# Attention on one core: value matmuls of two steps side by side in every second step, and a ring of 16 tiles of exponentials

## The chip, the core and the metric

The kernel runs on one core of one Trainium2 chip. A core has five engines that work at the same time, each on a queue of its own and in the order of that queue: TensorE (PE, matrix multiplication), VectorE (DVE), ScalarE (ACT), GpSimd (POOL) and SyncE (SP, which issues the transfers). They meet through semaphores: an instruction waits until another engine has counted far enough. The metric is the device time of one execution in microseconds (us); lower is better.

## What is computed

Two layers act on 16 images of 32 channels and 64 by 64 pixels. The first is a capsule layer with routing, the second a transformer block on 3x3 patches; each begins with a group normalization and adds its result to its input. The change lies in the attention of the second layer. Cut to that:

```python
xr = x @ Wr.T                                   # patches of 288 numbers to 144
qkv = (xr @ Wqkv.T).reshape(B, N, 3, 8, 18)     # 8 heads of 18 numbers
q, k, v = (qkv[i].reshape(B, 8, 4, n, 18) for i in range(3))   # 4 chunks of n = 1024 pixels
attn = softmax(einsum('bhcnd,bhcmd->bhcnm', q, k) * 18 ** -0.5)
o = einsum('bhcnm,bhcmd->bhcnd', attn, v)
out = o.reshape(B, N, 144) @ Wp.T + bp
```

## The kernel before

The program is five phases with a barrier behind each: a normalization, the routing, a normalization, the attention and a last phase for the MLP and the folding of the patches. Only `attention_phase` is touched.

**Units and steps.** The attention works through 64 units, one for each image and chunk (16 x 4). A unit is 32 steps: 2 groups of four heads ("quads") x 2 halves of 512 queries x 8 blocks of 128 keys. In step t, PE makes four score matmuls (`score`, x = 0 to 3, one per head, 128 keys x 512 queries, bf16), ACT makes the exponentials of each (`exponentials`), and the value matmuls (`values`) multiply these four tiles of exponentials by the values of their heads and add them up in `po`. The value matmuls are f32 and have 32 columns each, so the four stand beside each other in the array, each in a quarter of its columns; the trace shows eight matmul rows for one call. Before the scores of a unit, the greatest score of each row must be known, so the kernel makes every score twice: in each step PE also makes four matmuls for the maxima of the unit after it (`maximum`), and DVE reduces each of them (`TENSOR_REDUCE`).

**The order on PE** is written out by hand in `unit`: score 0, maximum 0, score 1, maximum 1, score 2, maximum 2, the value matmuls of the step before, score 3, maximum 3, and then the task of this step, if it has one. Here a "block" is what stands between maximum 2 and score 3.

**Tasks** are the rest of the work of a unit, laid by a table on certain steps (a unit that it belongs to, its kind, its number):

```python
TASKS = {0: (0, "max", 1), 1: (-1, "turn", 3), 2: (-1, "back", 3),
         3: (-1, "out", 2), 4: (-1, "out", 3), 5: (-1, "out", 4),
         6: (2, "qk", 0), 7: (2, "qk", 1), 8: (2, "qk", 2), 9: (0, "turn", 0), 10: (0, "back", 0),
         11: (2, "qk", 3), 12: (2, "qk", 4), 14: (1, "v", 0), 15: (1, "v", 1),
         16: (1, "v", 2), 17: (0, "turn", 1), 18: (0, "back", 1), 19: (1, "max", 0),
         25: (0, "turn", 2), 26: (0, "back", 2), 27: (0, "out", 0), 28: (0, "out", 1)}
```

So steps 13, 20 to 24 and 29 to 31 have no task. All tasks write one PSUM tile, `pm`, and PE starts a task only when the reader of the task before has taken `pm` out (`reader_before`, and the table `readers` above it). For "turn", "back", "out" and "qk" that reader is DVE, for "v" and "max" it is ACT. DVE does its part of the task of step t-1 in step t, between the second and the third reduction (`if x == 1: task(p, t - 1, which)` in DVE's `unit`).

**Buffers between the engines.** Scores go through 3 PSUM tiles (`sc`), maxima through 3 others (`mp`): the score with number k waits until the exponential of number k - 3 is done, the maximum with number k until the reduction of number k - 3 is done (`bank_before`). The exponentials lie in a ring of 8 tiles of 512 f32 (`ex`), two steps' worth; the first exponential of step t waits until the value matmuls of step t - 2 are done. Every eighth step ACT also copies `po` out into `oc` (`outputs`, L1429), behind the four exponentials of that step; the next value matmuls that start `po` anew wait for it.

Of the kernel before, what the change touches and what calls it, by code (L numbers as in the profile page):

```python
# [951 lines left out]
QUAD = 4  # L952
QUADS = HEADS // QUAD
STEPS = QUADS * QB * KB
# [5 lines left out]
NPART = 3  # L960
BANKS = 3
PER_UNIT = QUAD * STEPS


def bank_before(k):

    if k >= BANKS:
        return k - BANKS + 1
    return max(j for j in range(PER_UNIT - BANKS, PER_UNIT) if j % BANKS == k % BANKS) - PER_UNIT + 1

# [22 lines left out]
def offset(p, d):  # L993

    for _ in range(abs(d)):
        p = p.to(1 if d > 0 else -1)
    return p


def attention_phase(nc, ctx, sems, halves, ln_halves, mixed, moments, w_r, w_qkv, w_p, consts):  # L1000
# [10 lines left out]
    def sb(n, shape, dt=F32):  # L1011
        return ctx.enter_context(nc.sbuf_tensor(f"a_{n}", shape, dt))

    def sem(n):
        sems.append(nc.alloc_semaphore(f"a_{n}"))
        return sems[-1]
# [20 lines left out]
    mleft = sb("mleft", [128, 2, QUAD * KB])  # L1037
    mparts = sb("mparts", [128, NPART, QUAD * KB], BF16)
    mrow = sb("mrow", [NPART * QUAD * KB, 128], BF16)
    RING = 2 * QUAD  # L1040
    ex = sb("ex", [128, RING, CHUNK])
    oc = sb("oc", [128, CHUNK])
    rz = sb("rz", [128, BLK * QUAD])
# [41 lines left out]
    valued = Signal(sem("valued"), STEPS)  # L1085
# [15 lines left out]
    def piece(k, part):  # L1101

        if k == OUTS - 1:
            return packed[:, part, :]
        return pieces[:, k % WIDE, part, CHUNK * (k // WIDE):CHUNK * (k // WIDE + 1)]

    def width(k):
        return NARROW if k == OUTS - 1 else CHUNK
# [136 lines left out]
    def _(pe):  # L1245
# [69 lines left out]
        def score(p, t, x):  # L1315

            quad, qb, kb = t // 16, t // 8 % 2, t % 8
            k = QUAD * t + x
            head = QUAD * quad + x
            if t % 16 == 0 and x == 0:  # L1320
                pe.wait_ge(neg_in[quad].sem, neg_in[quad].at(p.n, 16))

            if not (isinstance(p.n, int) and p.n == 0 and k < BANKS):
                pe.wait_ge(exped.sem, exped.at(p.n, bank_before(k)))
            pe.matmul(sc[k % BANKS][:, :], ks[0:KROWS + NPART, p.h, head, 128 * kb:128 * kb + 128],  # L1325
                      qs[0:KROWS + NPART, p.h, head, CHUNK * qb:CHUNK * qb + CHUNK],
                      start=True, stop=True).then_inc(score_made.sem, 1)

        def maximum(p, t, x):

            k = 4 * t + x
            head, q = divmod(k // 2, KB)
            half = x % 2
            if k % (2 * QUAD * KB) == 0:
                pe.wait_ge(stack_in[head // QUAD].sem, stack_in[head // QUAD].at(p.n, 16 * 12))
            pe.wait_ge(maxed.sem, maxed.at(p.n, bank_before(k)))
            pe.matmul(mp[k % BANKS][:, :], qs[0:KROWS, p.h, head, 128 * q:128 * q + 128],  # L1337
                      ks[0:KROWS, p.h, head, CHUNK * half:CHUNK * half + CHUNK],
                      start=True, stop=True).then_inc(max_made.sem, 1)

        def values(p, t):

            quad, qb, kb = t // 16, t // 8 % 2, t % 8
            g = t // 8
            pe.wait_ge(exped.sem, exped.at(p.n, QUAD * t + QUAD))
            if t == 0:
                pe.wait_ge(v_done.sem, v_done.at(p.n, 3))
            if kb == 0 and not (isinstance(p.n, int) and p.n == 0 and g == 0):
                pe.wait_ge(o_copied.sem, o_copied.at(p.n, g))
            for x in range(QUAD):  # L1350
                last = pe.matmul(po[32 * x:32 * x + 32, :], va[:, p.h, kb, QUAD * quad + x, :],  # L1351
                                 ex[:, (QUAD * t + x) % RING, :], start=kb == 0, stop=kb == KB - 1,
                                 tile_position=(0, 32 * x))
            last.then_inc(valued.sem, 1)

        def unit(p, which):
            for t in range(STEPS):
                for x in range(QUAD):
                    if 0 in which:
                        score(p, t, x)  # L1360
                    if 1 in which:
                        maximum(p.to(1), t, x)
                    if x == 2 and t == 0 and -1 in which:
                        values(p.to(-1), STEPS - 1)
                    elif x == 2 and t and 0 in which:
                        values(p, t - 1)
                task(p, t, which)

        run_units(pe, units, unit)

    @block.scalar
    def _(act):
        for sig in (*t1_stored, spared, neg_spared, *mo_stored):
            act.sem_inc(sig.sem, sig.base)
        nc.scalar.preload_act_table_set(EXP_LN)
        for i in range(3):
            act.wait_ge(combined, i + 1)
            nc.scalar.copy(wc[:, i, :], pm[0:R, 0:3 * C2]).then_inc(wc_copied, 1)
        act.wait_ge(prepared, 1)

        def task(p, t, which):
            if t not in TASKS or TASKS[t][0] not in which:
                return
            d, kind, k = TASKS[t]
            own = offset(p, d)
            if kind == "qk":
                if k == 0:
                    act.wait_ge(spared.sem, spared.at(own.n, 0))
                act.wait_ge(qk_made.sem, qk_made.at(own.n, k + 1))
                nc.scalar.copy(piece(k, 0), pm[:, 0:width(k)]).then_inc(lead.sem, 1)  # L1390
            elif kind == "v":
                nb = min(3, KB - 3 * k)
                act.wait_ge(v_made.sem, v_made.at(own.n, k + 1))
                nc.scalar.copy(va[:, own.h, 3 * k:3 * k + nb, :, 0:HD],
                               pm[:, 0:C2 * nb].rearrange("p (b h d) -> p b h d", h=HEADS, d=HD)).then_inc(v_done.sem, 1)
            elif kind == "max":
                act.wait_ge(neg_turned.sem, neg_turned.at(own.n, k + 1))
                act.wait_ge(neg_spared.sem, neg_spared.at(own.n, 16 * k))
                nc.scalar.copy(mrow[:, :], pm_b[0:96, 0:128]).then_inc(neg_copied.sem, 1)

        def late_task(p, t, which):

            if t not in TASKS or TASKS[t][0] not in which:
                return
            d, kind, k = TASKS[t]
            own = offset(p, d)
            if kind == "qk":
                act.wait_ge(remain.sem, remain.at(own.n, k + 1))
                nc.scalar.copy(piece(k, 1), left[:, k % 2, 0:width(k)]).then_inc(second.sem, 1)  # L1409
            elif kind == "out":  # L1410
                act.wait_ge(t1_done.sem, t1_done.at(own.n, k + 1))
                if not (isinstance(own.n, int) and own.n == 0 and k == 0):
                    act.wait_ge(sq_done.sem, sq_done.at(own.n, k))
                nc.scalar.activation(sqr[:, 0:width(k)], t1[:, k, 0:width(k)], ACT.Square,
                                     accum_out=mo[:, own.h, OUTS + k:OUTS + k + 1]).then_inc(sq_done.sem, 1)

        def exponentials(p, t, pair):
            for x in range(2 * pair, 2 * pair + 2):
                k = QUAD * t + x
                act.wait_ge(score_made.sem, score_made.at(p.n, k + 1))  # L1420
                if x == 0 and not (isinstance(p.n, int) and p.n == 0 and t < 2):
                    act.wait_ge(valued.sem, valued.at(p.n, t - 1))
                nc.scalar.activation(ex[:, k % RING, :], sc[k % BANKS][:, :], ACT.Exp, scale=scale).then_inc(exped.sem, 1)  # L1423

        def outputs(p, g):
            act.wait_ge(valued.sem, valued.at(p.n, 8 * g + 8))
            if not (isinstance(p.n, int) and p.n == 0 and g == 0):
                act.wait_ge(o_normed.sem, o_normed.at(p.n, g))
            nc.scalar.copy(oc[:, :], po[:, :]).then_inc(o_copied.sem, 1)  # L1429

        def unit(p, which):
            for t in range(STEPS):
                if 0 in which:
                    exponentials(p, t, 0)
                    exponentials(p, t, 1)
                if t == 0 and -1 in which:
                    outputs(p.to(-1), 3)
                elif t and t % 8 == 0 and 0 in which:
                    outputs(p, t // 8 - 1)
                late_task(p, t - 1, which)  # L1440
                task(p, t, which)

        run_units(act, units, unit)
# [461 lines left out]
```

## Time and profile before

| | |
|---|---|
| median of 3 runs | 13064.68 us (13056.39 to 13068.2) |
| the profiled execution | 13060.79 us, span 13059.0 us |
| PE busy over the span | 12449.1 us, 95% |
| DVE busy | 9722.8 us, 74% |
| ACT busy | 7866.5 us, 60% |
| first and last value matmul | 4547.9 and 12248.0 us from the span's start |
| mean granted clock of PE | 0.982 of 2.4 GHz |

Busy time counts a matmul from its start to its modelled end, and matmuls overlap, so 95% does not say that PE streams data 95% of the time. In the rows below, the start of a matmul and the start of the next one tell what the first one costs; a duration is longer than that, by the time in which a result drains. The same holds in a lesser measure for DVE and ACT, whose next instruction starts before the end of the one before.

### The profile page before, as it was taken

How to read it: one execution, taken by the hardware profiler on the slowest of the kernel's cores; microseconds unless marked ns; L12 is line 12 of the kernel's file. 1: busy time of each engine (PE TensorE's matmuls, PEld its weight loads, DVE VectorE, ACT ScalarE, POOL GpSimd, SP SyncE). 2: the span in 40 equal slices, each digit the busy share in tenths (PEclk: the TensorE clock that was granted, in tenths of full speed). 3: DMA queues.
4: the chain of work that ended last, by engine and by line, in shares of the span. 5: the costliest groups of instructions: out<-in, count | busy, mean ns of one | idle time of the engine just before them, and what ended most of it. 6: DMA issues, size and time to landing. Idle time of an engine off the chain costs nothing. (4 is left out here: it accounts for less than half of the span.)

```text
span 13059.0 us, 258656 instructions
## 1 busy us (share of the span) xinstructions
PE 12449.1 (95%) x76092; PEld 5276.3 (40%) x76348; DVE 9722.8 (74%) x18034; ACT 7866.5 (60%) x14774; POOL 2684.0 (21%) x2692
## 2 busy tenths in 40 slices
PE   6999999999996499999999999999999999999899
PEld 3555555555553133333333333333333333333233
DVE  7888888888887577777777777777777777777311
ACT  4666666666665166666666666666666666666411
POOL 3454444544443000000000000000000000000143
PEclk9999999999998699999999999999999999999999
DMA  3101011010112523223222232332322323223255
GB/s 77 22 15 22 17 20 22 15 22 15 22 21 55 132 64 75 66 66 73 66 70 69 67 72 66 73 70 64 75 66 67 72 66 71 68 69 72 64 124 109
DMA packets 853225, 771.45 MB, mean 59 GB/s; under 512 B 587076, under 2 KB 621348, under 8 KB 840740
## 3 DMA queue, kind: packets, MB, share of 16 engines
q1 hardware_dynamic: 850468, 747.29, 25.4%
q8 instruction: 703, 11.52, 0.4%
q10 hardware_dynamic: 1536, 8.39, 0.3%
q14 instruction: 518, 4.24, 0.1%
HBM read 510.50 MB, written 244.96 MB: 58 GB/s over the span
## 5 line engine op out<-in xcount | busy, mean ns | idle before, releaser
L1503 DVE TENSOR_REDUCE a_big<-a_mp 128x1 f32<-128x512 f32 x8192 | 5222.3, 685 | 1816.0 <-PE a_mp L1337 1797.7
L1423 ACT ACTIVATE a_ex<-a_sc 128x512 f32<-128x512 f32 x8192 | 4426.4, 601 | 1937.6 <-PE a_sc L1325 1932.6
L1337 PE MATMUL a_mp<-a_ks,a_qs 108*128 108x512 bf16 x8192 | 3131.1, 383 | 39.9 <-DMA a_ks<-qk_parts 25.1
L1325 PE MATMUL a_sc<-a_qs,a_ks 111*128 111x512 bf16 x8192 | 3124.5, 383 | 6.8 <-ACT a_ex L1423 4.5
L849 DVE TENSOR_TENSOR r_prod<-r_pg,r_win 128x512 f32<-128x512 f32 x3584 | 2319.4, 683 | 416.5 <-PE r_pg L583 227.9
L1351 PE MATMUL a_po<-a_ex,a_va 128*32 128x512 f32 x16384 | 2183.0, 605 | 2.1 <-ACT a_oc L1429 0.7
L1239 POOL TENSOR_TENSOR a_pieces<-a_left,a_pieces 128x512 bf16<-128x512 f32 x256 | 295.5, 1154 | 7319.5 <-ACT a_pieces L1409 7319.5
L1325 PEld LDWEIGHTS a_sc<-a_qs,a_ks 111*128 111x128 bf16 x8192 | 794.9, 97 | 2477.6 <-ACT a_ex L1423 1767.0
L524 POOL TENSOR_TENSOR r_prod<-r_temp,r_win 128x512 f32<-128x512 f32 x1024 | 1214.7, 1207 | 1298.3 <-PE r_pl L632 568.3
L587 PE MATMUL r_pg<-r_ident,r_spread 128*128 128x128 f32 x9216 | 1196.7, 278 | 113.3 <-DVE r_prod L849 94.5
L587 PEld LDWEIGHTS r_pg<-r_ident,r_spread 128*128 128x128 f32 x9216 | 1004.9, 142 | 573.0 <-DVE r_prod L849 275.1
L1337 PEld LDWEIGHTS a_mp<-a_ks,a_qs 108*128 108x128 bf16 x8192 | 803.2, 98 | 913.6 <-DVE a_big L1503 237.7
L807 ACT ACTIVATE r_spread<-r_low 128x2048 f32<-128x2048 f32 x512 | 952.1, 1916 | 0.0
L582 PE MATMUL r_pg<-r_stack,r_wv 96*128 96x512 bf16 x2304 | 882.3, 383 | 28.4 <-DVE r_prod L849 10.1
L583 PE MATMUL r_pg<-r_stack,r_wv 128*128 128x512 bf16 x2048 | 778.4, 380 | 0.0
L1269 PE MATMUL a_pm<-a_zw,a_wc 96*128 96x512 f32 x1536 | 711.1, 599 | 15.1 <-DVE a_left L1473 13.4
L1351 PEld LDWEIGHTS a_po<-a_ex,a_va 128*32 128x32 f32 x16384 | 322.5, 107 | 824.7 <-ACT a_ex L1423 702.6
L629 PE MATMUL r_ps<-r_prod,r_ws 128*32 128x512 f32 x4096 | 553.3, 613 | 22.8 <-DVE r_prod L849 15.6
L1808 DVE TENSOR_TENSOR f_u<-f_pw,f_three 96x512 f32<-96x512 f32 x128 | 87.9, 687 | 651.4 <-PE f_pw L1677 650.1
L790 ACT COPY r_temp<-r_pg 128x512 f32<-128x512 f32 x1024 | 544.1, 583 | 20.4 <-ACT r_out_t L775 20.4
L632 PE MATMUL r_pl<-r_prod,r_pick 128*32 128x512 f32 x4096 | 541.1, 600 | 5.3 <-DVE r_prod L849 0.3
L1723 ACT ACTIVATE f_hidden<-f_ph,f_coef 72x512 f32<-72x512 f32 x128 | 99.0, 773 | 652.2 <-PE f_ph L1667 652.2
(192 smaller groups left out, 11795.2 us busy)
## 6 DMA issues: line engine op xcount, KB each, us to landing
a_qs<-qk_parts SPq DMA_DIRECT2D x768, 144.0 KB
a_ks<-qk_parts SPq DMA_DIRECT2D x768, 144.0 KB
qk_parts<-a_pieces SPq DMA_DIRECT2D x128, 768.0 KB, 5.0
f_t<-mixed SPq DMA_DIRECT2D x48, 1536.0 KB, 16.7
a_tw<-second SPq DMA_DIRECT2D x512, 128.0 KB, 3.1
mixed<-a_t SPq DMA_DIRECT2D x256, 256.0 KB, 2.1
r_win<-first SPq DMA_DIRECT2D x128, 280.5 KB, 5.2
a_zw<-layered SPq DMA_DIRECT2D x192, 144.0 KB, 12.2
```

The costliest lines, as they stand in the source:

```text
L524: nc.gpsimd.tensor_tensor(prod[:, g, :].rearrange("p (a b) -> p a b", b=IMG), temp[:, rank, :].rearrange("p (a b) -> p a b", b=IMG), tap_a ...
L582: pe.matmul(bank[:, :], wv_0[0:96, w], stack[0:96, lane, :], start=True, stop=False)
L583: last = pe.matmul(bank[:, :], wv_12[:, w], stack[:, lane, :], start=False, stop=True)
L587: last = pe.transpose(bank[:, 128 * b:128 * b + 128], spread[:, lane, 16 * kk:16 * kk + 16, :].rearrange("p a b -> p (a b)"), ident[:, :])
L807: nc.scalar.activation(to[:, :, half, :], src[:, :, half].unsqueeze(3).to_broadcast([128, BLK, 64, CLEN]), ACT.Exp).then_inc(prob[r].sem, 1)
L849: nc.vector.tensor_tensor(prod[:, g, :].rearrange("p (a b) -> p a b", b=IMG), pg[use % RINGS][:, :].rearrange("p (a b) -> p a b", b=IMG), ...
L1269: last = pe.matmul(pm[:, :], wc[:, i, 128 * (k % WIDE):128 * (k % WIDE) + 128], zw[:, own.h, first:first + CHUNK], start=i == 0, stop=i == 2)
L1325: pe.matmul(sc[k % BANKS][:, :], ks[0:KROWS + NPART, p.h, head, 128 * kb:128 * kb + 128], qs[0:KROWS + NPART, p.h, head, CHUNK * qb:CHUNK ...
L1337: pe.matmul(mp[k % BANKS][:, :], qs[0:KROWS, p.h, head, 128 * q:128 * q + 128], ks[0:KROWS, p.h, head, CHUNK * half:CHUNK * half + CHUNK], ...
L1351: last = pe.matmul(po[32 * x:32 * x + 32, :], va[:, p.h, kb, QUAD * quad + x, :], ex[:, (QUAD * t + x) % RING, :], start=kb == 0, stop=kb ...
L1423: nc.scalar.activation(ex[:, k % RING, :], sc[k % BANKS][:, :], ACT.Exp, scale=scale).then_inc(exped.sem, 1)
L1503: nc.vector.tensor_reduce(big[:, x % 2, k // 2:k // 2 + 1], mp[k % BANKS][:, :], AX_X, ALU.max).then_inc(maxed.sem, 1)
```

## The change

The value matmuls no longer stand in every step. In every even step t the block now holds those of steps t - 2 and t - 1, one after the other; in an odd step nothing stands between maximum 2 and score 3. For the last two steps of a unit they stand in step 0 of the next. The ring of exponentials has 16 tiles in place of 8 (four steps' worth), and the first exponential of step t now waits for the value matmuls of step t - 4. What is multiplied and in which order it is added up in `po` stays, and so do the orders of DVE, POOL and SP. ACT's order stays but for its waits.

```diff
+BATCH = 2
+RING_STEPS = 2 * BATCH
-    RING = 2 * QUAD
+    RING = RING_STEPS * QUAD
                     if x == 2 and t == 0 and -1 in which:
-                        values(p.to(-1), STEPS - 1)
-                    elif x == 2 and t and 0 in which:
-                        values(p, t - 1)
+                        for done in range(STEPS - BATCH, STEPS):
+                            values(p.to(-1), done)
+                    elif x == 2 and t and t % BATCH == 0 and 0 in which:
+                        for done in range(t - BATCH, t):
+                            values(p, done)
-                if x == 0 and not (isinstance(p.n, int) and p.n == 0 and t < 2):
-                    act.wait_ge(valued.sem, valued.at(p.n, t - 1))
+                if x == 0 and not (isinstance(p.n, int) and p.n == 0 and t < RING_STEPS):
+                    act.wait_ge(valued.sem, valued.at(p.n, t - RING_STEPS + 1))
```

In the orders below, L1325 and L1337 of before are L1327 and L1339 of after, and so on, since the change adds two lines above them (four on DVE and ACT); a_sc, a_mp, a_po, a_pm are the PSUM tiles `sc`, `mp`, `po`, `pm`, the digit behind `sc` and `mp` is the buffer.

PE before, from the task "out" of step 4 to the task "out" of step 5:

```order
L1305 MATMUL a_pm<-a_on,a_wp 128x512 x2
L1325 MATMUL a_sc2<-a_qs,a_ks 128x512
L1337 MATMUL a_mp2<-a_ks,a_qs 128x512
L1325 MATMUL a_sc0<-a_qs,a_ks 128x512
L1337 MATMUL a_mp0<-a_ks,a_qs 128x512
L1325 MATMUL a_sc1<-a_qs,a_ks 128x512
L1337 MATMUL a_mp1<-a_ks,a_qs 128x512
L1351 MATMUL a_po<-a_ex,a_va 32x512 x4
L1325 MATMUL a_sc2<-a_qs,a_ks 128x512
L1337 MATMUL a_mp2<-a_ks,a_qs 128x512
L1310 MATMUL a_pm<-a_on,a_wp 32x256 x8
```

PE after, the same place:

```order
L1307 MATMUL a_pm<-a_on,a_wp 128x512 x2
L1327 MATMUL a_sc2<-a_qs,a_ks 128x512
L1339 MATMUL a_mp2<-a_ks,a_qs 128x512
L1327 MATMUL a_sc0<-a_qs,a_ks 128x512
L1339 MATMUL a_mp0<-a_ks,a_qs 128x512
L1327 MATMUL a_sc1<-a_qs,a_ks 128x512
L1339 MATMUL a_mp1<-a_ks,a_qs 128x512
L1327 MATMUL a_sc2<-a_qs,a_ks 128x512
L1339 MATMUL a_mp2<-a_ks,a_qs 128x512
L1312 MATMUL a_pm<-a_on,a_wp 32x256 x8
```

The block of the odd step is gone, and eight score and maximum matmuls are all that stands between two tasks.

DVE at the same place, before: its part of the task of step 4, between the reductions of step 5.

```order
L1503 TENSOR_REDUCE a_big<-a_mp2 128x1
L1503 TENSOR_REDUCE a_big<-a_mp0 128x1
L1496 SCALAR_TENSOR_TENSOR a_t1,a_mo<-a_pm,a_tw 128x512
L1503 TENSOR_REDUCE a_big<-a_mp1 128x1
L1503 TENSOR_REDUCE a_big<-a_mp2 128x1
```

And after:

```order
L1507 TENSOR_REDUCE a_big<-a_mp2 128x1
L1507 TENSOR_REDUCE a_big<-a_mp0 128x1
L1500 SCALAR_TENSOR_TENSOR a_t1,a_mo<-a_pm,a_tw 128x512
L1507 TENSOR_REDUCE a_big<-a_mp1 128x1
L1507 TENSOR_REDUCE a_big<-a_mp2 128x1
```

Nothing moved on DVE: the part of the task still stands behind the second reduction of the step after it.

PE before in steps 20 and 21, which have no task, from block to block:

```order
L1351 MATMUL a_po<-a_ex,a_va 32x512 x4
L1325 MATMUL a_sc2<-a_qs,a_ks 128x512
L1337 MATMUL a_mp2<-a_ks,a_qs 128x512
L1325 MATMUL a_sc0<-a_qs,a_ks 128x512
L1337 MATMUL a_mp0<-a_ks,a_qs 128x512
L1325 MATMUL a_sc1<-a_qs,a_ks 128x512
L1337 MATMUL a_mp1<-a_ks,a_qs 128x512
L1325 MATMUL a_sc2<-a_qs,a_ks 128x512
L1337 MATMUL a_mp2<-a_ks,a_qs 128x512
L1351 MATMUL a_po<-a_ex,a_va 32x512 x4
```

And after, from the block of step 20 on:

```order
L1353 MATMUL a_po<-a_ex,a_va 32x512 x8
L1327 MATMUL a_sc2<-a_qs,a_ks 128x512
L1339 MATMUL a_mp2<-a_ks,a_qs 128x512
L1327 MATMUL a_sc0<-a_qs,a_ks 128x512
L1339 MATMUL a_mp0<-a_ks,a_qs 128x512
L1327 MATMUL a_sc1<-a_qs,a_ks 128x512
L1339 MATMUL a_mp1<-a_ks,a_qs 128x512
L1327 MATMUL a_sc2<-a_qs,a_ks 128x512
L1339 MATMUL a_mp2<-a_ks,a_qs 128x512
L1327 MATMUL a_sc0<-a_qs,a_ks 128x512
L1339 MATMUL a_mp0<-a_ks,a_qs 128x512
```

Eight calls stand together in place of four, and eight pairs of a score and a maximum follow before the next block (three more than shown) in place of four.

## Rows read from the trace of the kernel before

**Rows 1.** The page: busy time, share of the span, instructions of each engine.

```profile
PE 12449.1 (95%) x76092; PEld 5276.3 (40%) x76348; DVE 9722.8 (74%) x18034; ACT 7866.5 (60%) x14774; POOL 2684.0 (21%) x2692
```

**Rows 2.** Windows: length, busy time by engine (instructions), clock, DMA share, GB/s.

```profile
4520.00:4540.00 20.00, 20.00 (x35) 3.54 (x34) 20.00 (x35) 0.00 (x0) 0.00 (x0) 0.50 0.60 112
6000.00:12000.00 6000.00, 5991.48 (x33365) 2278.24 (x33365) 4562.04 (x8162) 3924.10 (x7766) 264.36 (x250) 1.00 0.30 69
```

**Rows 3.** Waits from 6000 to 12000 us: total, times, longest.

```profile
PE a_mp L1337 <- DVE a_big L1503: 6.8, 24, 0.3
```

**Rows 4.** Groups, 6000 to 12000 us: count, busy us, mean ns, idle before.

```profile
L1423 ACT ACTIVATE a_ex<-a_sc 128x512 f32<-128x512 f32 x6327 | 3420.5, 601 | 1489.1 <-PE a_sc L1325 1485.9
```

**Rows 5.** Timeline, a step without a task: start, us, engine, line, what, how many.

```profile
8138.66 0.38 PE L1337 MATMUL a_mp<-a_ks,a_qs 108*128 108x512 bf16 x1
8138.97 1.06 PE L1351 MATMUL a_po<-a_ex,a_va 128*32 128x512 f32 x8
8139.96 0.39 PE L1325 MATMUL a_sc<-a_qs,a_ks 111*128 111x512 bf16 x1
8140.19 0.38 PE L1337 MATMUL a_mp<-a_ks,a_qs 108*128 108x512 bf16 x1
8140.39 2.09 ACT L1423 ACTIVATE a_ex<-a_sc 128x512 f32<-128x512 f32 x4 [0.76 <-PE a_sc L1325]
8140.61 1.89 DVE L1503 TENSOR_REDUCE a_big<-a_mp 128x1 f32<-128x512 f32 x3 [0.36 <-PE a_mp L1337]
...
8141.28 0.38 PE L1325 MATMUL a_sc<-a_qs,a_ks 111*128 111x512 bf16 x1
8141.50 0.38 PE L1337 MATMUL a_mp<-a_ks,a_qs 108*128 108x512 bf16 x1
8141.81 0.64 PE L1351 MATMUL a_po<-a_ex,a_va 128*32 128x512 f32 x4
```

**Rows 6.** Timeline of PE around a task "qk" of three groups of four.

```profile
8106.22 0.38 PE L1337 MATMUL a_mp<-a_ks,a_qs 108*128 108x512 bf16 x1
8106.53 1.50 PE L1274 MATMUL a_pm<-a_zw,a_wc 96*32 96x256 f32 x24
8107.97 0.39 PE L1325 MATMUL a_sc<-a_qs,a_ks 111*128 111x512 bf16 x1
```

**Rows 7.** Timeline, from the task "out" of step 3 to that of step 4.

```profile
8037.50 1.88 PE L1305 MATMUL a_pm<-a_on,a_wp 128*128 128x512 f32 x4
...
8039.22 0.38 PE L1325 MATMUL a_sc<-a_qs,a_ks 111*128 111x512 bf16 x1
...
8039.85 1.29 DVE L1503 TENSOR_REDUCE a_big<-a_mp 128x1 f32<-128x512 f32 x2 [1.46 <-PE a_mp L1337]
...
8041.06 0.68 DVE L1496 SCALAR_TENSOR_TENSOR a_t<-a_pm,a_tw 128x512 f32<-128x512 f32 x1
...
8042.06 1.45 PE L1305 MATMUL a_pm<-a_on,a_wp 128*128 128x512 f32 x3
```

**Rows 8.** Timeline, first units, where PE makes maxima and tasks alone.

```profile
4469.47 0.68 DVE L1473 TENSOR_TENSOR a_left<-a_pm,a_pieces 128x512 f32<-128x512 f32 x1
...
4470.21 2.84 PE L1269 MATMUL a_pm<-a_zw,a_wc 96*128 96x512 f32 x6 [0.77 <-DVE a_left L1473]
...
4473.31 1.29 DVE L1503 TENSOR_REDUCE a_big<-a_mp 128x1 f32<-128x512 f32 x2 [1.96 <-PE a_mp L1337]
...
4474.06 0.39 PE L1337 MATMUL a_mp<-a_ks,a_qs 108*128 108x512 bf16 x1 [0.36 <-DVE a_big L1503]
```

**Rows 9.** Timeline of PE: the same task "qk" without a wait ahead.

```profile
8083.60 2.74 PE L1269 MATMUL a_pm<-a_zw,a_wc 96*128 96x512 f32 x6
```

**Rows 10.** Timeline of ACT around a copy of `po`.

```profile
8028.06 0.60 ACT L1423 ACTIVATE a_ex<-a_sc 128x512 f32<-128x512 f32 x1 [0.76 <-PE a_sc L1325]
8028.56 0.58 ACT L1429 COPY a_oc<-a_po 128x512 f32<-128x512 f32 x1
8029.02 1.60 ACT L1423 ACTIVATE a_ex<-a_sc 128x512 f32<-128x512 f32 x3
```

## The prediction

> **What bounds the kernel now.** I read the page first: PE is busy for 95% of the span [rows 1]. The windows say the same of the stretch that the change touches, which is the attention in its steady part: 5991 of 6000 us, at a granted clock of 1.00, which is 2.4 GHz [rows 2]. Of the waits, those of PE for DVE come to 6.8 us in 6000 [rows 3], so nothing else ends last there. The 6327 exponentials in that window, at 128 per unit, make 121.4 us per unit [rows 4]. Whoever takes time off PE's queue gains it, so long as ACT and DVE still keep up; whoever lets PE wait loses it.
>
> The timeline of a step without a task gives the prices. A score and a maximum start .22 us apart [rows 5], so a pair costs .44. From the last maximum ahead of a block to the score behind it 1.30 us pass (.31 + .99), of which .22 are that maximum, so a block costs 1.08 to 1.09. The step has four pairs and one block, and takes 2.84 [rows 5]. How much of the block is streaming follows from a task "out": two f32 calls of the same 512 columns take 1.72 us (8037.50 to 8039.22) [rows 7], .86 for one. The four value matmuls lie side by side and stream together, so they need .86 once, and about .23 of a block is a price for entering and leaving it.
>
> **The change: what it saves.** Two blocks become one with twice the streaming. Whether the price is then paid once or twice shows in the task "qk" that has three groups of four such matmuls in a row: 1.75 us from the maximum ahead to the score behind, less .22, is 1.53 [rows 6]. Half the columns take half of .86, so three groups stream for 1.29, and .24 is left for all three. The price is paid per stay, not per group, and each pair of steps saves .23: 32 steps x 64 units / 2 = 1024 times, or 236 us. That would be 12,825 us.
>
> The three groups of [rows 6] leave no room for a pause between one and the next: 1.29 of streaming and .24 are all of it. The Trainium skill ("TensorE: Matmul & The Clock Gate", section "Part 3: Packing small matmuls — row/col tiling", The mechanism) says that loading weights overlaps with matmuls in flight only when they use other rows of the array; the groups here all use the same 128 rows. By that rule the second group would pay for its entry again and the saving would be 0 in place of 236; the trace disagrees, with .24 for three groups of half the width.
>
> **What it adds: a wait for the one tile of the tasks.** All tasks write `pm`, and the next one starts only when the one before has been read, for most kinds by DVE, behind its second reduction of the next step. Rows 7 show one such step from its start S, the end of the task "out" of step 3 (8039.22): DVE reduces from S + .63, each .605 after the last, takes `pm` out from S + 1.84 and is done at S + 2.52. PE comes to the next task at S + 2.84. The wait is hidden by .32, and what hides it is the block. In an odd step of the changed kernel the block is gone: PE is there at S + 2.84 - 1.09 = S + 1.75. It may go on .06 after DVE's end (4473.31 + 1.29 - .60 = 4474.00 for a reduction, 4474.06 for the maximum that waited for it [rows 8]), so at S + 2.58. That is a wait of .83. DVE can't be sooner: its two reductions depend on maxima that PE makes in that same step, and it was idle before them (1.46 us in [rows 7]). Behind PE's wait stand the scores and maxima of the next step, so ACT and DVE wait with it and nothing makes it up. Starting again costs something too: the six matmuls of a task "qk" take 2.84 when PE had to wait for `pm` [rows 8], and 2.74 when not [rows 9]. With this .10 one wait costs .93.
>
> By the table, an odd step with a task whose predecessor stands in the step before and is read by DVE is 3, 5, 7, 9, 11, 19 and 27: seven per unit. (15 and 17 follow a "v", 1 a "max", both read by ACT, which is quicker; 25 follows no task.) Without the first two of the first unit, the three that hang on "qk" in the next to last, and all seven of the last, which has no maxima to reduce, 436 are left: 436 x .93 = 405 us.
>
> **What it adds: bursts that three tiles can't hold.** Between blocks there now stand eight pairs in place of four. PE makes one in .44, DVE reduces one in .605, and the maximum number j must wait for the reduction number j - 3, which ends .685 after its start. With a start of DVE .42 behind the maximum's (8140.19 to 8140.61 [rows 5]), eight pairs without a task go like this: reductions start at .42, 1.02, 1.62, 2.22 and 2.82; maxima 4 to 7 may start .745 behind reductions 1 to 4, at 1.77, 2.37, 2.97 and 3.57; PE alone would have been at 3.08. That loses .49, and the block of 1.95 that follows is too long for DVE to work through: three tiles are 1.8 us of work. Before, with four pairs, the first that could wait is the last, and the block comes in time.
>
> Two bursts of a unit are of this kind (blocks 20 to 22 and 22 to 24): .98. In the one from 28 to 30, a task stands behind the first pair, DVE idles, and then it has the 512 columns of that task to take out between the second and third reduction of the other seven; the same working gives .93. In the one from 12 to 14, with the half-size part of a "qk", it gives .65. ACT loses twice: it needs .50 for an exponential and .46 for the copy of `po` behind it [rows 10], and a score waits for the exponential three before, which ends .60 + .06 after its start. In the burst from step 24 score 4 would come at 1.75 and may come at .43 + .50 + .46 + .66 = 2.05 or a little later: .32. Across the seam of two units the burst from 30 to 0 would lose .49, and ACT's copies .42 in step 1; but part of the waits of [rows 3] may lie there already and go away, so I count half of the two, .45, an estimate. Sum: .98 + .93 + .65 + .32 + .45 = 3.33 per unit, times 63 units with maxima, 210 us. Bounds: half of it, if DVE and ACT are a little ahead of what I assume, and half more. In the last unit ACT's exponentials at .49 alone fill the steps and the double block starves it; I put 10 us there, an estimate.
>
> **What costs nothing.** The waits of the value matmuls themselves: score 2 of step t may start only when the exponentials of step t - 1 are all done, and this is what the block behind it waits for, for either of its two steps. The ring's wait moves from step t - 2 to t - 4, whose values were multiplied a step or more ago. The copy of `po` stands where it stood, a block ahead of the values that need it. No transfer, no instruction of POOL or SP moves; the other four phases are as they were.
>
> **Sum:** -236 + 405 + 210 + 10 = +389. On the profiled execution's 13060.8 us that is 13,450. It lies 4 us under the median of the runs, which is no matter here.
>
> **The rivals.**
> - *The groups of a stay pay one by one*, because the weights of the second group wait for the matmuls of the first: the waits stay, the saving does not, 13,450 + 236 = 13,686. Against it stands the stay of three groups [rows 6]. Chance 6%. It is what the Trainium skill's page "TensorE: Matmul & The Clock Gate" (Part 3, The mechanism) would have here.
> - *The wait for `pm` is hidden, not slower.* Its place is the odd steps; it decides whether DVE has read `pm` by S + 1.69 and not at S + 2.52. Then 405 us go: 13,045, within .2% of before. For it: DVE has idle time in these steps. Against it: this idle time lies ahead of the reductions that DVE must make first. Chance 5%.
> - *Neither wait costs*, and the saving is all there is: 12,825. It would need the three tiles to hold eight pairs; with .605 against .44 they don't. Chance 2%.
> - *PE's clock falls.* Where PE made one maximum per reduction, before the first scores, the granted clock was .50, which is 1.2 GHz [rows 2]. In the changed kernel PE would stream for some nine tenths of the time; there it had one matmul of .22 in each .60. A unit at half clock would take some 240 us in place of 127, so a tenth of the units would add some 700: 14,150. Chance 2%.
> - The change doing nothing is out: the order of PE is seen to differ in every step.
>
> **How the numbers follow.** The forecast, 13,450, has 85%. Its lower end is half the bursts and no price for starting again: 13,450 - 105 - 44 = 13,300. Its upper end is bursts half as costly again, 13,555, and a little for what the shifted orders may add at the seams of units: 13,575. The range 13,300 to 13,575 leaves the rivals out, and with them some 5% of the forecast's own case. A measurement of this kernel can tell about .2%, 26 us, from no change. Faster: 2%, and 1% of the second rival. Same: 4%. Slower: the rest, 93%.
>
> **What the changed kernel's profile would show.** A unit would take about 127.6 us in place of 121.4. PE would wait for the readers of `pm` (DVE L1500, L1489, L1477) in seven odd steps per unit, .8 us each; before, no such wait is in the list. Maxima would wait for reductions in steps 14, 22, 24, 30 and 0, some 3 us per unit in place of 6.8 us in fifty units. A block would take 1.95. If it took 2.17, the first rival holds. If PE came to the odd tasks without waiting, the step on `pm` is wrong, and most of the forecast with it.

## The result, and the profile after

The changed kernel took 13461.1 us (median of 4 runs, 13457.22 to 13465.7) where the one before took 13066.01: a ratio of 1.0305, with a 95% interval of 1.0292 to 1.0317. The forecast was 13,450, in a range of 13,300 to 13,575.

The page of the profiled execution, its span and its line of busy times, to be laid beside [rows 1]:

```profile
span 13456.4 us, 258940 instructions
PE 12451.7 (93%) x76348; PEld 5418.4 (40%) x76348; DVE 9691.7 (72%) x18034; ACT 7792.6 (58%) x14774; POOL 2686.8 (20%) x2692
```

The window of 6000 to 12000 us, beside [rows 2] (length, busy time and instructions by engine, clock, DMA share, GB/s):

```profile
6000.00:12000.00 6000.00, 5686.60 (x31766) 2269.80 (x31765) 4324.78 (x7769) 3683.54 (x7395) 250.32 (x237) 1.00 0.28 66
```

PE is busy for as long as before, at the same clock, and the span is 397 us longer: what was added is waiting. (The saving does not show in the busy time: a doubled block is busy for 1.92 us below, where two single ones were for 2 x 1.06 [rows 5], but the profile counts short waits as busy, as the last section shows.) In the window PE stands idle for 313 us in place of 9. The group of exponentials there, which [rows 4] show with x6327, has become smaller:

```profile
L1427 ACT ACTIVATE a_ex<-a_sc 128x512 f32<-128x512 f32 x6028 | 3180.9, 605 | 1694.0 <-PE a_sc L1327 1687.0
```

6028 exponentials are 47.1 units, so a unit takes 127.4 us; before it took 121.4, and 127.6 was forecast. The list of PE's waits in the same window, which had the one row of [rows 3], now reads (total, times, longest):

```profile
PE a_pm L1307 <- DVE a_on L1489: 71.4, 94, 0.8
PE a_mp L1339 <- DVE a_big L1507: 48.9, 118, 0.6
PE a_pm L1289 <- DVE a_on L1489: 35.1, 47, 0.7
PE a_pm L1294 <- DVE a_left L1477: 33.2, 47, 0.7
PE a_pm L1312 <- DVE a_t L1500: 31.8, 47, 0.7
PE a_pm L1271 <- DVE a_on L1489: 31.4, 47, 0.7
PE a_pm L1271 <- DVE a_left L1477: 29.6, 47, 0.6
PE a_sc L1327 <- ACT a_ex L1427: 25.5, 94, 0.5
```

The rows with `a_pm` are tasks that wait for DVE to read `pm`: 94 + 5 x 47 = 329 waits in 47 units, seven per unit, on tasks whose predecessor is "back" (`a_on`), "qk" (`a_left`) or "out" (`a_t`). These are the seven odd steps of the forecast. The row with `a_mp` is of maxima that wait for a reduction, the last one of scores that wait for an exponential.

One of the seven in the timeline, step 3, to be laid beside [rows 7] (start, us, engine, line, what, how many, idle time of the engine ahead of it):

```profile
8221.75 0.38 PE L1339 MATMUL a_mp<-a_ks,a_qs 108*128 108x512 bf16 x1
8222.07 0.68 DVE L1489 TENSOR_TENSOR a_on<-a_pm,a_oc 128x512 f32<-128x512 f32 x1
8222.66 1.28 DVE L1507 TENSOR_REDUCE a_big<-a_mp 128x1 f32<-128x512 f32 x2
8222.90 1.95 PE L1307 MATMUL a_pm<-a_on,a_wp 128*128 128x512 f32 x4 [0.76 <-DVE a_on L1489]
8224.69 0.38 PE L1327 MATMUL a_sc<-a_qs,a_ks 111*128 111x512 bf16 x1
```

The last maximum of the step starts at 8221.75, and the task could follow .22 later. DVE takes `pm` out only from 8222.07 to 8222.75, and the task starts at 8222.90. It then needs 1.79 to the next score in place of the 1.72 of [rows 7].

And PE between two blocks without a task, from step 22 to step 24, beside [rows 5]:

```profile
8332.40 0.39 PE L1339 MATMUL a_mp<-a_ks,a_qs 108*128 108x512 bf16 x1
8332.72 1.92 PE L1353 MATMUL a_po<-a_ex,a_va 128*32 128x512 f32 x16
8334.58 0.39 PE L1327 MATMUL a_sc<-a_qs,a_ks 111*128 111x512 bf16 x1
...
8336.80 0.38 PE L1327 MATMUL a_sc<-a_qs,a_ks 111*128 111x512 bf16 x1
8337.17 0.39 PE L1339 MATMUL a_mp<-a_ks,a_qs 108*128 108x512 bf16 x1
8337.40 0.38 PE L1327 MATMUL a_sc<-a_qs,a_ks 111*128 111x512 bf16 x1
8337.77 0.39 PE L1339 MATMUL a_mp<-a_ks,a_qs 108*128 108x512 bf16 x1
...
8338.68 1.92 PE L1353 MATMUL a_po<-a_ex,a_va 128*32 128x512 f32 x16
```

The doubled block costs .32 + 1.86 - .22 = 1.96, less than two of 1.09. But the pair of steps takes 5.96 where two single steps took 2 x 2.84 = 5.68: the late maxima follow their score by .37 and not by .22. DVE reduces all eight without a pause and paces them, one in .60:

```profile
8335.23 4.87 DVE L1507 TENSOR_REDUCE a_big<-a_mp 128x1 f32<-128x512 f32 x8 [1.09 <-PE a_mp L1339]
```

### The profile page after: what moved, and what is told of

It reads as the page before. It is cut to its first block and busy times, and to the rows that moved or that the text cites. A ratio compares the mean times of both kernels' runs of the same rounds, so it can differ in the third digit from the quotient of the medians.

```text
span 13456.4 us, 258940 instructions
## 1 busy us (share of the span) xinstructions
PE 12451.7 (93%) x76348; PEld 5418.4 (40%) x76348; DVE 9691.7 (72%) x18034; ACT 7792.6 (58%) x14774; POOL 2686.8 (20%) x2692
## 5 line engine op out<-in xcount | busy, mean ns | idle before, releaser
L1427 ACT ACTIVATE a_ex<-a_sc 128x512 f32<-128x512 f32 x8192 | 4320.0, 606 | 2314.3 <-PE a_sc L1327 2304.5
L1339 PE MATMUL a_mp<-a_ks,a_qs 108*128 108x512 bf16 x8192 | 3137.4, 383 | 98.5 <-DVE a_big L1507 73.3
L1327 PE MATMUL a_sc<-a_qs,a_ks 111*128 111x512 bf16 x8192 | 3121.8, 382 | 52.8 <-ACT a_ex L1427 40.8
L1353 PE MATMUL a_po<-a_ex,a_va 128*32 128x512 f32 x16384 | 1970.3, 598 | 0.1
L1327 PEld LDWEIGHTS a_sc<-a_qs,a_ks 111*128 111x128 bf16 x8192 | 794.6, 97 | 1798.3 <-issue 1018.8
L1339 PEld LDWEIGHTS a_mp<-a_ks,a_qs 108*128 108x128 bf16 x8192 | 799.2, 98 | 1299.9 <-DVE a_big L1507 665.0
L583 PE MATMUL r_pg<-r_stack,r_wv 128*128 128x512 bf16 x2304 | 876.5, 380 | 0.0
L1353 PEld LDWEIGHTS a_po<-a_ex,a_va 128*32 128x32 f32 x16384 | 427.4, 109 | 981.3 <-ACT a_ex L1427 586.3
L1271 PE MATMUL a_pm<-a_zw,a_wc 96*128 96x512 f32 x1536 | 729.2, 611 | 96.1 <-DVE a_left L1477 53.0
L1307 PE MATMUL a_pm<-a_on,a_wp 128*128 128x512 f32 x1024 | 490.8, 601 | 96.7 <-DVE a_on L1489 95.9
```

The costliest lines, as they stand in the source:

```text
L583: last = pe.matmul(bank[:, :], wv_12[:, w], stack[:, lane, :], start=False, stop=True)
L1271: last = pe.matmul(pm[:, :], wc[:, i, 128 * (k % WIDE):128 * (k % WIDE) + 128], zw[:, own.h, first:first + CHUNK], start=i == 0, stop=i == 2)
```

## Experiments

Differences are taken against the kernel before on the same chip. The diffs are cut to the lines that matter. Where the text gives waits "by the distances between starts", it takes PE's matmuls in the trace, from one start to the next, as means of units 5 to 59 (counted from 0); what a distance has above that of [rows 5] is a wait, also where the list of waits shows none. The theory was that of the forecast: doubled blocks save .23 us each, seven of sixteen make PE wait for `pm`, others make bursts that the three tiles of maxima can't hold. The rivals were that each doubled block costs the same wherever it stands, that the ring does, or that PE's pauses come from elsewhere.

**The ring alone.** Value matmuls in every step, as before:

```diff
-    RING = 2 * QUAD
+    RING = 4 * QUAD
-    act.wait_ge(valued.sem, valued.at(p.n, t - 1))
+    act.wait_ge(valued.sem, valued.at(p.n, t - 3))
```

> The kernel before with the ring of 16 tiles alone; the value matmuls stay in every step. Theory (the loss comes from the order on TensorE: waits for pm in odd steps, bursts between blocks): no change, 13,061 give or take 15 us, since ACT never waited for the ring before. Rival (the larger ring itself costs, through its place in memory or its longer reach): a good part of the 397 us, 13,200 or more.

Measured: 13058.03 against 13056.96, ratio 1.0002 (.9992 to 1.0011). The larger ring by itself costs nothing and gives nothing.

**The batch without the ring.** The changed kernel with `RING = 2 * QUAD` and the wait `t - 1`.

> The changed kernel with the ring left at 8 tiles: blocks of two steps, but the first exponential of step t waits again for the values of step t - 2. Theory: in every even step the exponentials can't start before the block of that same step is through, and score 3 waits for the first of them; about 1.2 us per pair of steps, 1024 times, so 14,300. Rival (the ring was never near its limit, the larger one is idle luxury): as the changed kernel, 13,458.

Measured: 13503.51 against 13056.96 (1.0341). This missed: 14,300 was expected, and it is only some 45 us more than the changed kernel (447 over before, in place of 395; 42 by the medians alone). The timeline around the block of a step 0 shows why:

```profile
8203.50 0.38 PE L1339 MATMUL a_mp<-a_ks,a_qs 108*128 108x512 bf16 x1
8203.81 1.92 PE L1353 MATMUL a_po<-a_ex,a_va 128*32 128x512 f32 x16
8204.94 2.06 ACT L1427 ACTIVATE a_ex<-a_sc 128x512 f32<-128x512 f32 x4 [1.81 <-PE a_po L1353]
8205.67 0.39 PE L1327 MATMUL a_sc<-a_qs,a_ks 111*128 111x512 bf16 x1
```

ACT does wait for the value matmuls, but only for the first group of the block: it starts 1.13 us into the 1.86 of the block. The first exponential runs from 8204.94 for .60 us beside the second group, and the score behind the block starts without delay. I had let ACT wait for the whole block. What is lost comes later: the scores wait for ACT once more per unit than the 94 times in 47 units of the list above.

```profile
PE a_sc L1327 <- ACT a_ex L1427: 59.6, 141, 0.5
```

By the distances between starts, a unit is longer than that of the changed kernel by .31 us in steps 0 to 2 and by .32 in steps 24 to 26, where ACT also copies `po`, and the last unit by 4.6: 44 us in all. So the ring of 16 is worth some 45 us here, no more.

**Undoing the batch where tasks wait.** Both kernels of this pair take a set of steps whose block is doubled; the others keep single blocks:

```diff
+PAIRED = (0, 2, 14, 16, 18, 22, 24, 26, 30)      # no_task_waits
+PAIRED = (4, 6, 8, 10, 12, 20, 28)               # no_bursts
-    elif x == 2 and t and t % BATCH == 0 and 0 in which:
-        for done in range(t - BATCH, t):
+    elif x == 2 and t and 0 in which and (t + 1) % STEPS not in PAIRED:
+        for done in range(t - (2 if t in PAIRED else 1), t):
```

> Values of two steps stand together only in steps 0, 2, 14, 16, 18, 22, 24, 26 and 30; around the seven odd steps in which a task follows one that DVE reads (3, 5, 7, 9, 11, 19, 27) each step has its own block again. Theory: the waits for pm go (405 us), of the saving 9 of 16 parts stay (133), and so do the bursts (210): 13,061 - 133 + 210 = 13,140. Rival (each doubled block costs the same, wherever it stands: 397 x 9 / 16 = 223): 13,284.

> The complement: values of two steps stand together only in steps 4, 6, 8, 10, 12, 20 and 28, behind the seven odd steps with a wait for pm. Theory: all seven waits stay (405), 7 of 16 parts of the saving (103), no bursts: 13,061 + 405 - 103 = 13,363. Rival (each doubled block costs the same: 397 x 7 / 16 = 174): 13,235.

Measured: 13155.01 (98 us over before) for the nine pairs without such a wait, 13364.12 (307 over) for the seven with it. Equal shares would have been 223 and 174; the theory had 79 and 302. The two add up to 405, and the whole change costs 395. The waits of PE in the window, first of the nine pairs, then of the seven:

```profile
PE a_mp L1340 <- DVE a_big L1508: 50.7, 122, 0.6
PE a_sc L1328 <- ACT a_ex L1428: 26.5, 98, 0.5
```

```profile
PE a_pm L1308 <- DVE a_on L1490: 73.0, 96, 0.8
PE a_pm L1290 <- DVE a_on L1490: 35.8, 48, 0.7
PE a_pm L1295 <- DVE a_left L1478: 33.2, 47, 0.7
PE a_pm L1313 <- DVE a_t L1501: 32.5, 48, 0.7
PE a_pm L1272 <- DVE a_on L1490: 31.4, 47, 0.7
PE a_pm L1272 <- DVE a_left L1478: 29.6, 47, 0.6
PE a_mp L1340 <- DVE a_big L1508: 6.8, 24, 0.3
```

Each half of the change has one half of the list: the nine pairs have the waits of maxima and scores and none on `pm`, the seven have those on `pm` and of the others only the 6.8 us of [rows 3].

**DVE reads `pm` sooner.** The blocks are as in the change, and DVE's part of a task is moved:

```diff
-                    if x == 1:
+                    if x == 0:                     # dve_sooner, dve_sooner_before
                         task(p, t - 1, which)
```

> The changed kernel with one thing moved: DVE does its part of a task behind the first reduction of the next step, not behind the second. Theory: DVE has read pm one reduction (.605 us) sooner, so each of the 436 waits falls from .83 to .23: 264 us less, 13,194; the moved part may lengthen some bursts, up to 13,240. Rival (TensorE's pauses in odd steps have another source than DVE's reading): 13,458.

> The kernel before with the same move: DVE's part of a task behind the first reduction. Theory: the block of each step hid this reading by .32 us, so nothing is gained: 13,061 give or take 20. Rival (the kernel before also lost time to the reading of pm): some 50 us or more faster.

Measured: 13233.76 against 13058.37 (1.0134), so 220 of the 395 us are gone, where 264 were expected and less if bursts became longer; with the same move the kernel before stays at 13057.05 (.9999, .9989 to 1.0008). On `pm` one row of waits is left:

```profile
PE a_mp L1339 <- DVE a_big L1507: 38.0, 121, 0.5
PE a_sc L1327 <- ACT a_ex L1427: 27.0, 98, 0.5
PE a_pm L1307 <- DVE a_on L1489: 16.0, 98, 0.2
```

One reduction sooner or later in DVE's reading is worth 220 us where the block of an odd step is gone, and nothing where it stands. The list tells only a part of it. By the distances between starts, the waits for `pm` fall from 6.0 to 1.8 us per unit. Five of the seven places become .60 shorter, that of step 9 .45, and that of step 19 only .09, because maxima wait there in turn, for .49. These two places are what is missing of the 264 (.66 per unit, 42 us).

**DVE reads `pm` as early as it can**, before the first reduction, for "qk" behind it:

```diff
+EARLY = {"qk": 1}
                 for x in range(4):
+                    if x == EARLY.get(TASKS.get(t - 1, (0, ""))[1], 0):
+                        task(p, t - 1, which)
                     if 1 in which:
                         maximum(p.to(1), t, x)
-                    if x == 1:
-                        task(p, t - 1, which)
```

> The changed kernel with DVE's part of a task moved as far ahead as it goes: before the first reduction of the next step, for tasks of kind qk (which need ACT first) behind it. Theory: four of the seven waits go wholly (.93 each), three fall to about .33, so 5.5 of 6.5 us per unit go; with the reductions pushed back a little in return 13,130 to 13,160. Rival (the waits are only exchanged for waits of the maxima on the delayed reductions): 13,300 or more.

Measured: 13158.23 against 13058.37 (1.0076). It takes 295 of the 395 us away, as forecast. The list of PE's waits in the window has no row on `pm` left, and a smaller one of maxima:

```profile
PE a_sc L1328 <- ACT a_ex L1428: 26.6, 98, 0.5
PE a_mp L1340 <- DVE a_big L1508: 14.6, 73, 0.2
```

The list misleads here. By the distances between starts, .5 us per unit of waits for `pm` are left (steps 7 and 9), and the waits of maxima have grown, from 3.0 us per unit in the changed kernel to 4.0; most are too short for the list. So some of the wait was exchanged, as the rival had it, but far less than was gained. What is left is slower than before by 100 us all the same.

**Reductions of half the width**, with the nine pairs of no_task_waits and, as a control, in the kernel before:

```diff
-    nc.vector.tensor_reduce(big[:, x % 2, k // 2:k // 2 + 1], mp[k % BANKS][:, :],
+    nc.vector.tensor_reduce(big[:, x % 2, k // 2:k // 2 + 1], mp[k % BANKS][:, 0:CHUNK // 2],
-    scale = float(HD) ** -0.5
+    scale = 0.25 * float(HD) ** -0.5
```

> As no_task_waits, with the reductions cut to half their width: half of each row of scores is left out of the maxima, and the factor inside the exponential is a quarter of its value, so the output is another. Theory: with .33 us per reduction DVE is faster than TensorE makes maxima (.44), so the bursts on mp go (2.6 of 3.3 us per unit, some 165 us less than no_task_waits): 12,965 to 12,980. Rival (the remaining loss lies with ACT or with the doubled block itself): as no_task_waits.

> The kernel before with the reductions cut to half their width (half of each row of scores left out of the maxima, the factor inside the exponential a quarter): the control for half_no_task_waits. Theory: TensorE hardly waited for reductions before (6.8 us in 6000), so 13,030 to 13,061; then nearly all of the 215 us between no_task_waits and half_no_task_waits are bursts that the doubled blocks made. Rival (shorter reductions help any order of this kernel, by less waiting at the seam of units): 12,950 or less.

Measured: 12939.71 with the nine pairs (119 under before, and 217 less than no_task_waits by these differences), and 13000.82 in the kernel before (64 under it; .995, .9933 to .9966). The control lies between theory and rival. Its window of 6000 to 12000 us:

```profile
6000.00:12000.00 6000.00, 5998.24 (x33540) 2291.96 (x33539) 3221.04 (x8210) 3947.84 (x7811) 263.71 (x250) 1.00 0.30 69
```

PE is idle for 2 us there, where it was for 9. The waits of PE in the same window with the nine pairs:

```profile
PE a_sc L1328 <- ACT a_ex L1428: 22.8, 100, 0.3
PE a_mp L1340 <- DVE a_big L1508: 5.8, 25, 0.2
```

So the kernel before did lose something to its reductions, 64 us in all. The theory had left out two places, which the traces show. From the first maximum to the first score, where PE makes maxima and tasks alone, 96.6 us became 72.2. And from the first score of the first unit to that of the last, 7621.4 us became 7582.3: .60 per unit, of which .50 lie in steps 0 to 2. The other 217 - 64 = 153 us (145 by the traces, over the same 63 units) are what the doubled blocks added in waits for reductions. With those gone, the nine pairs gain 55 over their control, of 9 x 63 x .23 = 130 that they save. The distances between starts say where the missing 75 us are: scores wait for ACT more than in the control, by .39 us per unit in steps 0 to 2, .30 in steps 24 to 26 and .22 in steps 30 to 0, and maxima by .25 in steps 28 to 30. Together this is 1.16 per unit, 73 us in 63 units.

**Doubled blocks only where nothing waits.** Two versions, the second without any change to DVE:

```diff
+PAIRED = (0, 4, 6, 12, 16, 18, 28)   # seven_paired, with EARLY as in dve_earliest
+PAIRED = (0, 16, 18)                 # three_paired, DVE as before
```

> Values of two steps stand together only in steps 0, 4, 6, 12, 16, 18 and 28, and DVE's part of a task comes before the first reduction of the next step (for kind qk behind it). Theory: seven of 16 parts of the saving (103 us), no wait for pm but small ones where the odd step follows back or out, .18 us of waits of maxima in steps 3, 11 and 27 (34 us): 13,061 - 103 + 34 = 12,992, and up to 13,015 by what dve_earliest lay over its forecast. Faster than both kernels. Rival (the saving of .23 per pair isn't there when nothing else changes): no faster than before, 13,061 or more.

> Values of two steps stand together only in steps 0, 16 and 18; all else as in the changed kernel, DVE's order included. No odd step with a wait for pm, no burst beyond that at the seam of two units. Theory: 3 x .23 x 63 = 43 us less than before, 13,018; without a gain at the seam 13,032. Rival (no saving per pair): 13,061.

Measured: 13004.83 against 13057.78, ratio .996 (.9946 to .9973), and 13022.87, ratio .9974 (.9964 to .9984). Both beat the kernel before, by 53 and 35 us, and the changed kernel by far more. The saving is there, and it is small. In three_paired the blocks of steps 16 and 18 save .24 us per unit each, and that of step 0 saves .1. The first one's waits of PE in the window:

```profile
PE a_sc L1329 <- ACT a_ex L1429: 15.4, 50, 0.5
PE a_mp L1341 <- DVE a_big L1509: 5.9, 26, 0.2
```

## Why the prediction was right, step by step

The terms of the forecast can be read off the traces of before and after one by one. The distance from the score behind the block of an even step to the score behind that of the next, after less before, mean of units 5 to 59, holds one doubled block and what it cost. Steps 14 to 16 and 16 to 18, where nothing else changes, are shorter by .24 each; this saving is added back to the others.

| us per unit | forecast | measured |
|---|---|---|
| saved by 16 doubled blocks | 3.68 | 3.84 |
| seven waits for `pm` | 6.51 | 6.53 (.75 to 1.00 each) |
| bursts 20 to 22 and 22 to 24 | .98 | 1.01 |
| burst 28 to 30 | .93 | .96 |
| burst 12 to 14 | .65 | .68 |
| ACT's copy of `po`, from step 24 | .32 | .31 |
| seam of two units, steps 30 to 2 | .45 | .53 |
| a unit becomes longer by | 6.16 | 6.18 |

- **The saving, 236 us.** Right: a doubled block costs 1.96 in the rows of step 22, where 1.95 was forecast. The sentence of the Trainium skill that the forecast rested its rival on ("TensorE: Matmul & The Clock Gate", "Part 3: Packing small matmuls — row/col tiling", The mechanism), read alone, would have given 2 x 1.09 = 2.18. The trace decides against it here, by that cost and by the weight loads of the same 128 rows, which run inside the block (step 4, changed kernel):

```profile
8226.09 1.92 PE L1353 MATMUL a_po<-a_ex,a_va 128*32 128x512 f32 x16
8226.54 0.13 PEld L1353 LDWEIGHTS a_po<-a_ex,a_va 128*32 128x32 f32 x4 [0.30 <-ACT a_ex L1427]
8226.97 0.13 PEld L1353 LDWEIGHTS a_po<-a_ex,a_va 128*32 128x32 f32 x4 [0.30 <-issue]
```

- **The wait for `pm`, 405 us.** Right in place, count and size. The places are the seven per unit in the rows on `pm`; no_bursts costs 307 with seven sixteenths of the saving (103) in it, so the waits cost 410. Of the .93 for one, .83 was forecast to be waiting and .10 a slower start; it is .85 and .08 in the mean of the seven. dve_sooner shows that DVE's reading is what PE waits for: it comes one reduction (.60) sooner and 220 us go. That the block of each step had hidden the reading for nothing is shown by dve_sooner_before, which gains nothing.
- **The bursts, 210 us.** Right: 3.49 per unit, 220 us, and each of them near its forecast. The burst of steps 22 to 24 loses 5.96 - 5.68 + .23 = .51 in the rows, where .49 was worked out. no_task_waits, with the same bursts and none of the waits for `pm`, costs 98 with nine sixteenths of the saving (133) in it, so by it the bursts and the last unit cost 231, where 220 were forecast. What was weakly founded is the seam, where half of .49 + .42 was counted, on the ground that some of the waits of [rows 3] might go away. In fact .64 came at steps 30 to 0 (maxima and scores) and .39 at steps 0 to 2 (scores that wait for ACT), while .50 of old waits of maxima in steps 0 to 2 went. Those old waits are far more than the .14 per unit that [rows 3] show; they stay in no_bursts and are gone in three_paired, so the doubled block of step 0 takes them away. The reason held, but that its half came within .08 is in part luck. At the seam one rule is also tighter than told ahead of the prediction: by `bank_before`, scores and maxima 0 and 1 of a unit wait for the second last before them, not the third last, since 128 is no multiple of 3.
- **The last unit, 10 us** and its share of the saving, 3.7, make 6.3. From its first score to its last value matmul the traces have 85.1 us before and 92.6 after: 7.6 more.
- **What was to cost nothing** cost nothing: the ring (ring_alone), the clock (1.00 in the window), the waits of the value matmuls (none in the list).
- **The sum.** 385 us in the 63 units and 7.6 in the last are 393 of the 397 us between the two traces. The other 4 lie ahead of the first score and behind the last value matmul, where the order is the same. So the agreement is not one of errors that cancel. The rivals each fall by one row: the price per group by the block of 1.96, the hidden wait by the rows on `pm`, that neither wait costs by the list again, the clock by the window. The reading on which the forecast priced the clock was loose: the row of 4520 to 4540 us [rows 2] has PE busy throughout, with 35 matmuls in 20 us, and .22 for one is a figure from rows at the higher clock.

## What to carry to other kernels

A fixed cost that is paid per change of work can be saved by standing like work together, and a stay of several groups elsewhere in the same trace tells beforehand how much. But the work that is moved was also time in which other engines caught up: before it is moved, go through every wait that it hides and see which is late next. Here the gain was .23 us per pair of steps, one hidden wait alone cost .93, and the change pays only at the places where no such wait stands.

## What was not expected of the hardware

- **The list of waits tells of PE's waits only in part.** It counts idle time from the modelled end of a matmul, which lies some .16 us behind the moment in which the next could start (a duration of .38 against a distance of .22 [rows 5]). So a wait of .15, as between 8337.40 and 8337.77 above, is in no list; the `a_mp` row of 48.9 us for 47 units makes 1.0 per unit, where the distances between starts make 3.0. The list of dve_earliest even fell while these waits grew.
- **Some tasks that waited for `pm` start later than a maximum that waited.** The maximum of [rows 8] came .06 behind DVE's end; the task of step 3 came .15 behind it (8222.75 to 8222.90) and was then .07 slower. The forecast had .06 and .10. Over the window of the changed kernel it is .15 for the tasks of L1307, .13 for those of L1289 and L1294, and .05 for those of L1271 and L1312. What makes the difference is not shown: L1271 and L1307 are both f32 with 128 columns of weights.
- **A group inside a doubled block signals at its own end**, while the next group streams: ACT started at 8204.94, .73 ahead of the score behind the block. This is why a ring of half the size costs some 45 us and not 840.
